# Three full expert slots run before the slot list of a fused GNN and mixture-of-experts kernel, with weights ringed by rank

## The reference, cut to what matters

```python
x = x + gnn(layernorm(x), edges)     # 1250 nodes x 768, 40000 edges
#   layer 1: GAT, 4 heads x 256, layer norm, relu, + h0 @ Wr1 + br1
#   layer 2: GAT, 1 head x 768, layer norm, + h1 @ Wr2 + br2
xf = layernorm(x)                    # no gain, no shift
gates = softmax(xf @ Wr + br)        # 8 experts
top_g, top_i = top_k(gates, 2)
for e in range(8):
    w_e = sum(top_g * (top_i == e))
    h = gelu(xf @ W1[e] + b1[e])     # 768 -> 384
    out += w_e * (h @ W2[e] + b2[e]) # 384 -> 768
x = x + out
```

## Time and profile before

| | us |
|---|---|
| median of 3 runs | 1165.88 |
| lowest, highest | 1160.1, 1169.18 |
| the profiled execution | 1167.09 |
| its span, first to last instruction | 1165.4 |
| PE busy | 1078.8 |
| DVE busy | 689.8 |
| mean granted clock of PE | 0.965 |

### The profile page before, as it was taken

How to read it: one execution, slowest core, us unless ns; L and a number is a source line. 1 busy time by engine, 2 the same in 40 slices (tenths; PEclk the granted TensorE clock), 3 DMA queues, 4 the chain that set the end, 5 groups by cost and what they waited for, 6 DMA issues and landing times.

```text
span 1165.4 us, 15149 instructions
## 1 busy us (share of the span) xinstructions
PE 1078.8 (93%) x4471; PEld 720.9 (62%) x4472; DVE 689.8 (59%) x1642; ACT 358.0 (31%) x628; POOL 137.2 (12%) x267
## 2 busy tenths in 40 slices
PE   5989999999899999989999999999996398998994
PEld 3457777664488888856556556656664255664662
DVE  5988889469467777878465416867776222322322
ACT  1222221243377777621001024810000122333331
POOL 3000000000000000011010000002222112323332
PEclk9989999999999999999999999999998599998998
...
GB/s 249 182 106 200 202 199 192 219 37 36 40 116 159 45 1 36 1 196 80 45 70 62 40 14 30 118 269 107 121 109 146 161 164 240 122 220 165 127 104 105
DMA packets 53132, 140.84 MB, mean 121 GB/s; under 512 B 8297, under 2 KB 16649, under 8 KB 52817
## 3 DMA queue, kind: packets, MB, share of 16 engines
...
## 4 chain that ended last, share of the span: by engine, by line
PE 44%; issue 36%; DMA 8%; DVE 7%; DVEq 2%; SPq 1%; POOL 1%; ACT 1%; ACTq 0%; POOLq 0%
PE PSA L1614 10%; PE PSA L1564 9%; PE PSA L1553 7%; PE PSA L1687 7%; PE PSA L1699 6%; DMA RW<-in_L_gnn_W 2%; DMA xs_d<-RB,RW2X 2%; DVE RW2X L771 2%; DMA RW<-out,RW 1%; DVE RB L785 1%; PE PSA L1676 1%; DMA out<-RW 1%; DVE RW2X L773 1%; DMA RW<-xs_d 1%; PE PSA L1634 1%
## 5 line engine op out<-in xcount | busy, mean ns | idle before, releaser
L1537 PE MATMUL PSA<-RW2X 125*125 125x257 f32 x800 | 175.6, 383 | 3.8 <-DVE RW2X L836 3.8
L1537 PEld LDWEIGHTS PSA<-RW2X 125*125 125x125 f32 x800 | 150.9, 189 | 28.9 <-issue 4.6
L1614 PE MATMUL PSA<-RW2X,RW 125*125 125x385 f32 (+1 forms) x360 | 122.4, 489 | 0.0
L1564 PE MATMUL PSA<-RW2X,RX 128*125 128x384 f32 x320 | 109.4, 498 | 1.0 <-DVE RW2X L914 1.0
L1375 PE MATMUL PSA<-RW,RX 128*125 128x512 f32 x240 | 108.4, 602 | 1.9 <-ACT RX L1114 1.9
L1392 PE MATMUL PSA<-RW,RX 128*125 128x512 f32 (+2 forms) x360 | 110.1, 460 | 0.0
L1687 PE MATMUL PSA<-RW2X,RW 128*128 (+1 forms) x276 | 101.6, 522 | 6.0 <-ACT RW L1303 6.0
L1553 PE MATMUL PSA<-RW2X,RX 128*125 128x384 f32 x320 | 105.1, 487 | 2.2 <-ACT RX L1224 1.4
L830 DVE TENSOR_TENSOR RW2X<-RW2X 125x625 f32<-125x625 f32 x80 | 64.8, 811 | 63.4 <-ACT RW2X L1213 63.2
L1213 ACT ACTIVATE RW2X<-RX,RK 125x625 f32<-125x625 f32 x120 | 91.5, 811 | 31.3 <-PE PSA L1537 31.3
L771 DVE TENSOR_SCALAR RW2X<-RW2X 125x250 bf16<-125x250 int16 x400 | 82.7, 281 | 22.6 <-issue 20.0
...
## 6 DMA issues: line engine op xcount, KB each, us to landing
...
```

Of the source, the lines that this page charges most:

```text
L1537: last = mm(ps[n % 7][0:TP, 0:XW], ering[:, (p * NT + m) % EBUF, 0, i * TP:(i + 1) * TP], xl[:, m, p // 2, :], start=(m == 0), stop=(m == ...
L1564: last = mm(ps[RB2[m]][0:TP, 0:D2], h1T[t % 3][:, kk, :], wr2s[:, kk, m * D2:(m + 1) * D2], start=(kk == 0), stop=(kk == K1 - 1))
L1614: last = mm(ps[PAIR[t % 3][c]][0:TP, 0:DW - c], p2[m][:, t * TP:(t + 1) * TP], xl2[:, m, c, 0:DW - c], start=(m == 0), stop=(m == NT - 1))
```

## The change

**Early slots.** When the counts of the first CUT = 6 tiles stand (in `d_rank(6)`), VectorE works out in `d_pos(6)`, with some 24 operations on one partition, which full groups of 128 rows exist by then, and takes the first EARLY = 3 of them, in order of experts. For these inputs that is one slot of expert 0 and two of expert 2. SP loads their rows, and the weights and first biases of their experts, at tile 8; `scatter(6)` waits for these row loads. The slots run under fixed program order on all engines, interleaved with the routing of tiles 8 and 9, and no longer as turns of the loop; the loop starts at slot 3. Their gets and puts are plain: put, wait for it, get. The slot list subtracts them; 23 slots stay, as 0 | 2, 2 | 0, 0 | 2 x4 | 1 | 4 x9 | 5 | 7 x3.

**Ring by rank.** The weight ring is filled in the order of ranks (experts with early slots first: 0, 2, 1, 3, ...), and expert numbers come from registers. No weights are loaded before the last stage of layer 2 any more.

**Order of the last tiles.** Tile 8 has a third buffer (xfr8), two scatters may be under way, tile 9's router uses PSUM bank 0, and tiles 8 and 9 are ranked after `add_b1(0)`. Buffers are laid out anew.

**Layer 1.** `norm_stats(3)` stands ahead of `wa1_sums`, no longer behind it.

```diff
+ALWAYS = (0, 2, 5)
...
+EARLY, CUT = 3, 6
+W0 = 4 * D
...
+RT = (NT - 1) * (7,) + (0,)
 ROUTE = (9, 18, 26, 34, 43, 51, 60, 69, 78)
...
-            load_expert(0)
-            load_expert(1)
             sp.wait_ge(prob2_ready, NT)
...
             for t in range(NT):
+                if t == CUT + 2:
+                    sp.wait_ge(early_ready, 1)
+                    who = [sp.value_load(early_i[0:1, 0, i:i + 1], min_val=0, max_val=E - 1) for i in range(EARLY)]
+                    first = [sp.value_load(early_i[0:1, 1, i:i + 1], min_val=0, max_val=E * CAP - 128)
+                             for i in range(EARLY)]
+                    ranked = [sp.value_load(who_i[0:1, j:j + 1], min_val=0, max_val=E - 1) for j in range(3)]
+                    for i in range(2):
+                        sp.wait_ge(rows_sent[i], 32 * (CUT // 2))
+                    for i in range(EARLY):
+                        sp.dma_start(xs[i], xs_d[ds(first[i], 128), :]).then_inc(xs_loaded, 16)
+                    for j in range(2):
+                        load_expert(j, ranked[j])
+                    sp.dma_start(fb1e[0], fb1[ds(who[0], 1), :].to_broadcast([128, FI])).then_inc(ld_fb1e, 16)
                 if t == NT - 1:
                     sp.wait_ge(row2_done, NT)
+                    for i in range(1, EARLY):
+                        sp.dma_start(fb1e[i], fb1[ds(who[i], 1), :].to_broadcast([128, FI])).then_inc(ld_fb1e, 16)
+                    load_expert(2, ranked[2])
                     sp.dma_start(fb1_bc.rearrange("p (e f) -> p e f", e=E),
                                  fb1[None].to_broadcast([128, E, FI])).then_inc(ld_fb, 16)
+                    for j in range(2):
+                        sp.wait_ge(w_in[j], 32)
+                        sp.sem_inc(w_ready, 1)
                 sp.wait_ge(x1_ready, t + 1)
...
+            sp.wait_ge(w_in[2], 32)
+            sp.sem_inc(w_ready, 1)
             sp.wait_ge(slots_ready, 1)
-            for e in range(2, E):
-                if e >= WRING:
-                    used = sp.value_load(slot_i[0:1, 2, e - WRING:e - WRING + 1], min_val=0, max_val=27)
+            row = sp.value_load(slot_i[0:1, 1, EARLY:EARLY + 1], min_val=0, max_val=E * CAP - 128)
+            for i in range(2):
+                sp.wait_ge(rows_sent[i], 32 * HT)
+            sp.wait_ge(xs_turned, 1)
+            sp.wait_ge(tg_kept, 1)
+            sp.dma_start(xs[0], xs_d[ds(row, 128), :]).then_inc(xs_loaded, 16)
+            sp.wait_ge(router_done, NT)
...
             def scatter(t):
-                if t:
-                    pool.wait_ge(rows_sent, 32 * t)
+                pool.wait_ge(rows_sent[t % 2], 32 * (t // 2))
                 pool.wait_ge(pos_ready, t + 1)
+                if t == CUT:
+                    pool.wait_ge(xs_loaded, 16 * EARLY)
                 for m in range(2):
                     g.indirect_dma_start(out=xs_d, out_offset=bass.IndirectOffsetOnAxis(ap=pos_all[:, t, m:m + 1], axis=0),
-                                         in_=xfr[t % 2], in_offset=None).then_inc(rows_sent, 16)
+                                         in_=row_of(t), in_offset=None).then_inc(rows_sent[t % 2], 16)
+            def hold(i):
...
+                    if t == NT - 1 and m == 0:
+                        pool.wait_ge(tg_kept, 1)
+                        g.tensor_copy(tok_g, tgr_i[:, 0:1])
+                        g.tensor_copy(tok_s, tgr_i[:, 0:1]).then_inc(tok_ready, 2)
+                        for i in range(2):
+                            pool.wait_ge(x1_stored[i], 32 * (CUT // 2))
+                        pool.wait_ge(tok_ready, 2)
+                        get_rows(out[0:CUT * TP, :], last_early)
...
+            for n in range(1, EARLY):
+                pool.wait_ge(tg_kept, n + 1)
+                pool.wait_ge(y_ready, n)
+                pool.wait_ge(tok_ready, n * 2)
+                put_rows()
+                at = n * (1 + E)
+                g.tensor_copy(tok_g, tgr_i[:, at:at + 1]).then_inc(tok_ready, 1)
+                pool.wait_ge(tok_ready, n * 2 + 1)
+                pool.wait_ge(y_stored, n * 16)
+                get_rows(out[0:CUT * TP, :], last_early)
+                g.tensor_copy(tok_s, tgr_i[:, at:at + 1]).then_inc(tok_ready, 1)
...
-                if p == 1:
-                    wa1_sums()
                 if t is not None:
                     if t == 2:
                         dve.wait_ge(ld_x, 32)
                     norm_stats(t)
+                if p == 1:
+                    wa1_sums()
...
+                if t == CUT:
+                    own.link(v.tensor_scalar(full8, ps[7][0:1, 288:296], 1.0 / 128, -0.498, ALU.mult, ALU.add))
+                    own.link(v.tensor_scalar(full8, full8, MAGIC, -MAGIC, ALU.add, ALU.add))
+                    own.link(v.tensor_tensor_scan(inc8, one8, full8, 0.0, ALU.mult, ALU.add))
...
+                    v.tensor_copy(early_i, early_f).then_inc(early_ready, 1)
...
+                if 1 <= t < NT - 1:
                     d_top(t - 1)
                 d_x1(t)
-                if t:
+                if 1 <= t < NT - 1:
                     d_pos(t - 1)
                 d_xf(t)
-            d_top(NT - 1)
-            d_pos(NT - 1)
+            dve.wait_ge(ld_fb1e, 16 * EARLY)
+            add_b1(0)
+            for t in (NT - 2, NT - 1):
+                d_top(t)
+                d_pos(t)
+            add_b1(1)
...
+            for t in range(NT):
+                if t < NT - 1:
+                    xf_keep(t)
+                if t == NT - 2:
+                    xs_keep(0)
+                    xs_keep(1)
...
+            gelu(0)
+            h_keep(0)
+            xs_keep(2)
+            act.wait_ge(ld_fb2, 16)
+            act.wait_ge(early_ready, 1)
+            act.wait_ge(rows_sent[0], 32 * HT)
+            gelu(1)
+            bias2(0)
+            h_keep(1)
+            bias2(1)
+            gelu(2)
+            h_keep(2)
             act.wait_ge(slots_ready, 1)
-            total = act.value_load(slot_i[0:1, 2, 7:8], min_val=1, max_val=27)
...
+            xs_turn(0)
+            d_logits(NT - 2)
+            mm1(0)
+            xs_turn(1)
+            d_route(NT - 1)
+            mm1(1, 0, 1)
+            d_rank(NT - 2)
+            d_logits(NT - 1)
+            mm1(1, 1, 4)
+            d_rank(NT - 1)
+            mm1(1, 4, KD)
+            h_turn(0)
+            xs_turn(2)
             pe.wait_ge(pos_ready, NT)
-            mm(ps[7][0:1, 0:8], ones[0:TP, 0:1], acum, start=True, stop=True).then_inc(count_done, 1)
-            def expert(n):
-                return pe.value_load(slot_i[0:1, 0, ds(n, 1)], min_val=0, max_val=E - 1)
-            def xs_turn(n):
-                pe.wait_ge(xs_loaded, 16 * (n + 1))
-                if not (isinstance(n, int) and n == 0):
-                    pe.wait_ge(xs_kept, 2 * n)
-                for kk in range(KD):
-                    last = tr(ps[kk // 4][:, (kk % 4) * 128:(kk % 4 + 1) * 128], xs[:, kk * 128:(kk + 1) * 128], ident)
-                last.then_inc(xs_turned, 1)
```

More of the change, by code:

```diff
@@ new lines, in mm2 @@
+            def mm2(n):
+                w0 = pe.snap((rank(n) % WRING) * WE + KD * FI, min_val=0, max_val=WRING * WE)
+                pe.wait_ge(h_kept, n + 1)
+                if isinstance(n, int) and n == 0:
+                    pe.wait_ge(pos_ready, NT - 1)
+                else:
+                    pe.wait_ge(y_drained, n)
+                for kk in range(KF):
+                    for c in range(2):
+                        last = mm(ps[M2[c]][:, 0:384], hT[:, kk, :], wbuf[:, ds(w0 + kk * D + c * 384, 384)],
+                                  start=(kk == 0), stop=(kk == KF - 1))
+                last.then_inc(mm2_done, 1)
```

414 lines of the change are left out of this document (254 added, 160 removed).

## The result

The changed kernel takes 1157.92 us (median of 20 runs, 1152.81 to 1168.57) against 1165.57 for the one before (20 runs, 1160.1 to 1172.15); the ratio is 0.9939 with a 95% interval of 0.992 to 0.9958, so 5 to 9 us faster, 7.1 by the ratio. The forecast was 1151. The profiled execution took 1156.89, its span is 1155.2.

What follows compares the result with a forecast made beforehand. PE, busy 93% of the span, was taken to set the pace, with idle holes in layer 1, ahead of slot 0 and at expert borders. -4.8 - 14.6 + 3.6 = -15.8 took 1167.09 to 1151.3, forecast 1151 us, range 1139 to 1167.

Steps and rivals of the forecast that it cites:

- Layer 1: Tile 3's statistics moved ahead: the counting product ends at 68.8 us, not 73.8; -4.8 us, bounds -3.8 and -6.5.
- Step 1: Seam, VectorE: the new block of some 24 small operations in `d_pos(6)` takes 4.9 us.
- Step 2: Seam, SP: nine register reads take 3 us together; three row loads issue from about 881.9 and land at 887.4.
- Steps 3 and 4: Seam: scatter(6) waits for the rows, tile 8's roots behind it; `d_xf(8)` +10.8 us at 896.8, `d_xf(9)` +8.6 at 909.5.
- Step 5: Seam: 8.4 MB from 882 at 305 GB/s land at 909.5; `mm1(0)`, needing only rank 0, runs 905.7 to 911.
- Step 8: Seam: puts and gets strictly in turn; adds at 932, 944, 955, 965; mm1(6) at 972 against 986.59, -14.6 us.
- Step 9: Behind mm1(6): weights loading at three borders between experts lose 14.5 us, against 10.9 before; +3.6 us.
- The transfers are the path: Rival, seam: at 182 GB/s weights land at 928 and rounds cost 14.9 us; 1178 us, slower; chance 0.12.
- Moved, not shortened: Rival, seam: row loads land at 902, +14.6 us, and only layer 1's gain is left; 1163 to 1166 us; chance 0.25.
- The seam closes: Rival, seam: cheap register reads, row loads at 885, rounds of 8.7 us give back some 12 us; 1139 us; chance 0.13.

Runs made afterwards that it cites:

- a_again: The changed kernel, unchanged, traced and timed again: 1156.33 us, 0.9933 of the kernel before.
- e2: The changed kernel with SP reading three registers ahead of the row loads and the other six after them: 1153.19 us, 0.9901 of the kernel before.
- e6: The changed kernel with rank 3's weights held back until slot 3's second product is done: 1154.73 us, 0.9926 of the kernel before.
- e10: The changed kernel with the statistics of tiles 2 and 3 behind the sums of W1 again: 1161.33 us, 0.9951 of the kernel before.
- e11: The changed kernel without the load of rank 3's weights, which no product of these inputs reads: 1157.32 us, 0.9896 of the kernel before.
- e1: The kernel before with only the statistics of tiles 2 and 3 ahead of the sums of W1: 1162.37 us, 0.9986 of the kernel before.
- e13: e8 with the statistics of tiles 2 and 3 behind the sums of W1: 1154.02 us, 0.9898 of the kernel before.
- e7: The changed kernel with weights of ranks 4 to 7 held until the first get behind their border has landed: 1155.57 us, 0.9927 of the kernel before.
- b_again: The kernel before, unchanged, run for a second trace: 1157.86 us in one execution.
- e3: The changed kernel with scatter(6) behind both roots of tile 8 on GpSimd: 1158.13 us, 0.9934 of the kernel before.
- e12: e8 with scatter(6) behind the roots of tile 8: 1148.24 us, 0.9864 of the kernel before.
- e5: The changed kernel with the edits of e2, e3 and e4 together: 1150.26 us, 0.988 of the kernel before.
- e4: The changed kernel with rank 0's weights handed over when in, and gelu(1) ahead of ScalarE's wait for scatter(8): 1153.64 us, 0.9913 of the kernel before.
- e8: The changed kernel with three register reads first and rank 3's weights held to the end of slot 3: 1150.50 us, 0.9859 of the kernel before.

## Why the prediction was wrong

It had the direction and the stretches right and forecast too much: -15.8 against -7.1 by the ratio, 1151 us against 1157.92. The measured stretches add up to nearly that: 3.0 us in the turn (mean of four traces with the old order, 80.33, and of fourteen with the new, 77.31), 7.6 in the seam (112.87 to 105.23), 3.2 lost again behind mm1(6) (153.22 to 156.44, the latter the mean of the changed kernel, a_again, e2 to e6, e10 and e11): -7.4. That is over the means; the pair on record has 3.2, 8.4 and 3.3. The stretch from the turn to layer 2 is left out of it: 456.6 in the mean of the three old traces and 458.1 of the fifteen others, within a spread of 454.0 to 462.3.

**Layer 1, forecast -4.8, measured -1.6 to -3.6** in three pairs of kernels (e1, e10, e13), -3.0 at the turn. The step that failed is "the product ends about 1.1 us after 67.7", where the forecast took the full clock for granted behind two new waits. PE was at the product at 64.37 (forecast 64.8) and the last one-hots let it go on at 68.04, as forecast. Behind them stand half of the product's 16 parts; at a granted clock of 0.50 they took 1.99 us, and the dense product that follows 6.07, not 5.50 as before. The same stretch in e2, behind the same two waits (0.62 and 1.56 us), has a clock of 1.00:

```profile
68.43 1.14 PE L1575 MATMUL PSA<-RW2X 125*125 125x250 bf16 x8 [1.56 <-DVE RW2X L854]
69.49 5.50 PE L1555 MATMUL PSA<-RW,RX 128*125 128x256 f32 x24
```

So it is in e6 and e7, and the turn of these three comes at 75.2 in the mean, 5.1 us ahead of the old order's 80.33: the forecast's gain, where the clock holds. In the other eleven traces with the new order the parts took 1.66 to 2.00 us, the dense product 6.07 to 7.55, and the turn comes at 77.9 in the mean. No run tests what decides between the two; the same kernel (a_again) shows 1.66 us once and 1.99 the other time. The 4.95 us that the pair on record shows at d_pos(6) looked like a hit, and b_again shows that 4.39 can come without the edit.

**Step 1, held**: some 4.5 us for the block (867.05 to 871.54), 4.9 forecast.

**Step 2, the step that failed at the seam.** "I take 3 together" for nine register reads, a term for which the prediction had no row. SP issued the first row load 5.86 us behind the residual load of tile 9 (873.06 to 878.92). In the old trace's clock (4.95 us on top) that is 883.9 in place of 881.9, and scatter(6), which waits for the rows, started 7.5 us later and not 5.5, with the weights issued close behind the rows: scatter(6) 4.0 late against the forecast, d_xf(8) 3.7 (900.5 against 896.8), d_xf(9) 3.8, the last `d_pos` 4.5, the slots 4. With six of the reads behind the row loads 3.5 to 4.6 us came back (e2).

**Steps 3 and 4, right in mechanism, but not the path.** The wait for scatter(6) held tile 8 as described. e3 and e12 show that without it PE waits instead for SP's hand-over of rank 0's weights (in e3 they had been in for 12 us), and e5 that an early mm1(0) doesn't bring an early mm1(6) either.

**Step 5.** The rate was better than my 305 GB/s (390 in the window 886 to 901), and rank 0's weights were in at 891.7, 896.6 in the old clock. The step took their landing for what mm1(0) waits for; mm1(0) at 910.3 in the old clock against a forecast 905.7 is step 2's lateness plus the hand-over behind the other issues, rank 2's weights among them. It ran at a granted clock of 0.58 (6.83 us), behind the hole of 886 to 901, and from 912 on, PE busy, the clock is 1.00. None of it reached mm1(6) (e4, e5).

**Step 8, the other term.** The first add came at 937.5 in the old clock (forecast 932: 4.0 from the slots, the rest ScalarE's bias, which stands behind gelu(1) and scatter(8)) and the second 14.9 us behind it, not 12. Rank 3's weights, issued at 934.07 behind slot 3's rows, lay on the first put; I had costed loads at the borders and none here. 14.9 stood in the prediction as the price of a round under a load; the forecast did not ask which load would be there. e11 prices it at 4.1 us on that round and 3.0 on the seam. mm1(6) came at 978.2 in the old clock and not 972.

**Step 9, held**: +3.2 against +3.6, with the three borders as described. The sum behind it was rough (three borders at two prices of 7.1), and the changed trace lost 3.8 us behind mm1(6) and 10.3 behind mm1(11) to mm1(13), 14.0 together against the 14.5 taken.

**The rivals.** *The transfers are the path* is refuted by 390 GB/s and by scatter(8), whose second half took 9.5 us (919.52 to 929.07, when gelu(1) could go), no more than the 9.48 of the earlier trace rows. Nor did the weights slow the scatters much, for which the prediction had no row: in e4 those of tiles 6 and 7, beside two experts' weights, landed 6.6 to 12.4 us behind their issue, 6.3 to 12.2 in the kernel before, without weights; in e5, issued closer together, 8.7 to 13.8. The rule behind the rival does hold for the first put and get. The Trainium skill (DMA: Bandwidth & Descriptors, Issuing engines are not separate DMA queues) has DMAs of all queues share the same 16 engines. The first rounds agree: 13.4 to 16.2 us beside the load, 9.6 to 11.1 without. *Moved, not shortened* came nearest in time, by another way: no row load landed at 902. *The seam closes* supposed cheap reads and 8.7 us rounds; e8, which comes near both, is 16 us faster than the kernel before, where the rival had 27.
